# The last group's recurrence, routing and dispatch tables, moved to later steps of the shared expert's loop

## What is computed

```python
x = x + attention(layernorm(x))
x = x + wkv(k=layernorm(x), v=context)       # per channel, a scan over the 128 tokens:
#   q = max(pp, u + k);  y = (exp(pp-q)*aa + exp(u+k-q)*v) / (exp(pp-q)*bb + exp(u+k-q))
h = layernorm(x)
probs = softmax(h @ router_w.T);  top 4 of 16, renormalised
routed = sum over the 4 picks of weight * down_e(silu(h @ gate_e) * (h @ up_e))
shared = silu(h @ sh_gate) * (h @ sh_up) @ sh_down
x = x + routed + sigmoid(h @ sh_gate_w) * shared
```

## Time and profile before

| | us |
|---|---|
| median of 3 runs | 1773.11 (1771.67 to 1774.23) |
| profiled execution, its own time | 1771.54 |
| its span | 1769.7 |
| shared expert's loop on PE | 611.0 to 763.8 |
| tile phase on PE | from 763.76 |

### The profile page before, as it was taken

The page is one execution under the profiler, slowest core; times in us unless marked ns, Lnnn a source line. Parts: engine busy times, 40 slices in busy tenths (PEclk is TensorE's granted clock), DMA queues, the critical chain, the costliest instruction groups (busy, mean ns, idle before and its releaser), DMA issues.

```text
span 1769.7 us, 26015 instructions
## 1 busy us (share of the span) xinstructions
PE 1595.4 (90%) x8599; PEld 1286.9 (73%) x8599; DVE 1115.7 (63%) x2506; ACT 948.8 (54%) x3002; POOL 554.8 (31%) x466
## 2 busy tenths in 40 slices
PE   6999999989998777899999879999879999999766
PEld 4888878878877655667777657777758888888534
DVE  3553675577577576454444475554467888877877
ACT  4666655556665643323323445676836565566556
POOL 2233332464255262411001664446131132211000
PEclk9999999999999988999999878998989999999988
DMA  8043234433354062144433410100031111000001
GB/s 269 27 167 129 95 114 137 158 125 111 123 177 141 22 173 69 60 121 123 130 105 115 146 59 28 34 4 25 1 140 31 33 42 34 12 1 1 1 1 48
DMA packets 85241, 147.33 MB, mean 83 GB/s; under 512 B 9700, under 2 KB 45172, under 8 KB 85108
## 3 DMA queue, kind: packets, MB, share of 16 engines
q1 hardware_dynamic: 78964, 128.89, 22.5%
q0 software_dynamic: 6144, 16.79, 3.0%
HBM read 86.65 MB, written 58.98 MB: 82 GB/s over the span
## 4 chain that ended last, share of the span: by engine, by line
PE 47%; DVE 9%; ACT 3%; issue 3%; POOL 1%; another core or an unknown queue 1%; DVEq 0%; POOLq 0%; ACTq 0%
PE bank L926 5%; PE bank L1163 5%; PE bank L620 4%; PE bank L622 4%; PE bank L944 4%; PE bank L621 4%; PE bank L1043 3%; PE bank L1154 3%; PE bank L1137 3%; PE bank L1025 3%; PE bank L1032 1%; PE bank L1126 1%; PE bank L1145 1%; PE bank L934 1%; PE bank L917 1%
## 5 line engine op out<-in xcount | busy, mean ns | idle before, releaser
L2673 ACT ACTIVATE cross_attention_heads<-cross_attention_heads,small 128x128 f32<-128x128 f32 x256 | 99.6, 390 | 117.7 <-DVE small L2075 117.7
L815 PE MATMUL bank<-self_attention 128*128 128x256 f32 x512 | 127.2, 393 | 21.6 <-ACT self_attention L2409 18.9
L1163 PE MATMUL bank<-cross_attention,cross_attention_heads 128*128 128x256 f32 x512 | 122.1, 381 | 12.8 <-DVE residual L2089 8.2
L2778 POOL CAST qkv_weights_split<-self_attention 128x1024 fp32r<-128x1024 f32 x45 | 51.0, 1133 | 254.8 <-DMA self_attention<-in_wqkv 229.8
L815 PEld LDWEIGHTS bank<-self_attention 128*128 128x128 f32 x512 | 99.5, 198 | 41.3 <-issue 21.7
L2393 ACT ACTIVATE self_attention<-self_attention,small 128x128 f32<-128x128 f32 x256 | 100.2, 394 | 46.6 <-DVE small L1706 43.6
L620 PE MATMUL bank<-x_channel_major,qkv_weights_split 128*128 128x512 f32 x256 | 116.9, 457 | 7.2 <-DVE qkv_weights_split L1739 2.9
L2585 ACT ACTIVATE narrow_late<-bank,small 128x128 f32<-128x128 f32 x256 | 91.2, 376 | 53.3 <-DVE small L1942 52.9
L1163 PEld LDWEIGHTS bank<-cross_attention,cross_attention_heads 128*128 128x128 f32 x512 | 96.0, 190 | 31.2 <-DVE residual L2089 15.1
L2780 POOL TENSOR_TENSOR qkv_weights_split<-self_attention,qkv_weights_split 128x1024 fp32r<-128x1024 f32 x45 | 110.5, 2456 | 3.7
L926 PE MATMUL bank<-experts,tiles 128*128 x316 | 108.0, 465 | 1.8 <-DVE tiles L1816 1.8
(11 more groups left out here) (408 smaller groups left out, 4640.4 us busy)
## 6 DMA issues: line engine op xcount, KB each, us to landing
picked_inputs<-self_attention SPq DMA_DIRECT2D x64, 512.0 KB, 6.3
self_attention<-in_wqkv SPq DMA_DIRECT2D x48, 512.0 KB, 6.1
experts_far<-picked_inputs SPq DMA_DIRECT2D x79, 128.0 KB, 2.1
picked_outputs<-tiles SPq DMA_DIRECT2D x79, 128.0 KB, 1.7
self_attention<-in_wo SPq DMA_DIRECT2D x16, 512.0 KB
experts<-in_moe SPq DMA_DIRECT2D x4, 1408.0 KB
context_values<-context_out SPq DMA_DIRECT2D x16, 256.0 KB
cross_attention<-context_values SPq DMA_DIRECT2D x4, 1024.0 KB, 8.8
```

The costliest lines, as they stand in the source:

```text
L815: m = T.matmul(bank[7][:, 0:D], ZT_a[n % 2][:, h, :], wo_a[p % 2][:, h, :], start=h == 0, stop=h == HG - 1)
L1163: m = T.matmul(bank[7][:, 0:D], ZT_x[n % 2][:, h, :], x_wo[hg % 2][:, h, :], start=h == 0, stop=h == HG - 1)
L2673: m = S.activation(P_x[u][:, h, :], P_x[u][:, h, :], ACT.Exp, bias=negmax_x[u][:, h:h + 1], accum_out=sums_x[u][:, h:h + 1])
```

## The change

Only the numbers of steps between pieces are changed, and on POOL the third scatter of group 2 now stands ahead of the first `wkv_helps`. The work is the same, and so are the units. The core of the diff, on PE, then a line or two of two other engines:

```diff
@@ PE last_group
-                yield from pause(3)
+                yield from pause(6)
                 last_keys(c)
                 yield from pause(5)
                 last_keys(c + 1)
+                yield from pause(6)
+                last_y(c)
+                yield from pause(7)
+                last_y(c + 1)
                 yield from pause(5)
-                last_y(c)
-                yield from pause(5)
-                last_y(c + 1)
-                yield from pause(4)
                 turn_xt(NORM["routing", g], 0)
@@ DVE last_group
                 normalised(NORM["wkv", g])
-                yield from pause(2)
+                yield from pause(5)
                 last_peak(c)
...
                 last_y(c + 1)
-                yield from pause(2)
+                yield from pause(5)
                 last_add(c + 1)
@@ POOL last_group
+                yield from pause(3)
+                scatter(NG - 2, 2)
                 yield from pause(2)
                 wkv_helps(KT * (NG - 1))
-                yield from pause(2)
-                scatter(NG - 2, 2)
```

More of the change, by code:

```diff
@@ L737, in last_group @@
                 logits(g)
-                yield
+                yield from pause(2)
                 turn_logits(g)
-                yield from pause(3)
+                yield from pause(4)
                 count_places(g)
@@ L2354, in last_group @@
                 last_more_exps(c + 1)
-                yield from pause(6)
+                yield from pause(10)
                 both_tables()
@@ L2824, in last_group @@
                 scatter(NG - 2, 1)
+                yield from pause(3)
+                scatter(NG - 2, 2)
                 yield from pause(2)
                 wkv_helps(KT * (NG - 1))
-                yield from pause(2)
-                scatter(NG - 2, 2)
                 yield from pause(3)
                 scatter(NG - 2, 3)
-                yield from pause(2)
+                yield from pause(4)
                 wkv_helps(KT * (NG - 1) + 1)
-                yield from pause(17)
+                yield from pause(21)
                 for b in range(GB):
```

## The result

The changed kernel took 1756.63 us (median of 6, 1751.94 to 1763.60), the kernel before 1772.33 in the same rounds (median of 6, 1770.11 to 1774.23). The ratio of the two is 0.9931, with a 95% interval of 0.9908 to 0.9954: 12 us faster by the ratio, 15.7 by the medians.

What follows compares the result with a forecast made beforehand. PE was taken to set the loop's end, the chain slots, scatter, load having 20.2 us to spare. After: slots 720.2 + 25.4 = tile start 745.6 against 763.76, 18.2 us earlier, so 1755 us; range 1750 to 1766.

Steps and rivals of the forecast that it cites:

- What PE has left after the slots: PE's work between slots and tile phase: 45.6 us before, 20.3 to 25.3 after the change.
- stall as that of unit 19: ACT's late gate near 740 in the kernel before, costing PE 5.0 us; it might or might not come back.
- the rival of the grown stall: Stall near the loop's end at twice 5.0 us: PE ends at 750.5, gain 13.3, 1759.8; chance 0.07.
- What the chain needs: From slots through sixteen scatters to the landed first tile load: unchanged at 25.4 us, now deciding the tile start.
- The slots at 720.2: Date when DVE writes the slots: 2 us later than the 718.19 before, with bounds 717.0 and 726.8.
- The start of the recurrence: DVE's first scan of the recurrence: at 630.3, 1.2 us earlier than before.
- (b): DVE's added products, low parts and sums ahead of the slots: 6.6 us, partly hidden, slots taken 2 later.
- The sum: Tile start 720.2 + 25.4 = 745.6 against 763.76 before: an 18.2 us shift, carried in full to the end.
- the 8.3 for y: PE's waits for y of the recurrence ahead of the slots: 8.3 us go by meeting y of d later.
- second entry: PE's wait for the normalised rows ahead of the slots: 7.5 us, of which 6.5 were to go.

Runs made afterwards that it cites:

- e2: The changed kernel with PE's two transposes of y at steps 17 and 23 instead of 18 and 25; ratio to before 0.9966.
- e4: The changed kernel with picks, slots, tables, count_places and last scatters four steps later on every engine; ratio to before 0.9981.
- e7: The changed kernel with keys, recurrence and y three steps earlier, POOL as before, routing kept at its steps; ratio to before 0.9975.
- e9: The changed kernel with POOL's helps of half c ahead of the third scatter again, fourth scatter at its old step; ratio to before 0.9901.
- e11: The kernel before with y of half d on PE, and all routing behind it on every engine, two steps later; ratio 1.0017.
- e1: The kernel before with the keys and all behind them three steps later on each engine, distances kept; 1742.82 us against 1754.98, ratio 0.9927.
- e8: e1 with both exponentials of d in one ACT unit, DVE's first scan one step later, y of d and routing two later; 1734.04 us, ratio 0.9901.
- e3: The changed kernel with 8 of the last 16 scatters, leaving half of the last group's tokens out of the experts; ratio to before 0.9882.
- e5: The changed kernel, unaltered, profiled on another chip; 1735.29 us against 1754.58, ratio 0.9922.
- e6: The kernel before, unaltered, profiled on the same other chip as e5; 1754.58 us.

## Why the prediction came out as it did

The sign and the path were right, and the time lies in the range: PE set the end of the loop before, 20 us behind the chain slots, scatter, load; the change moved PE's work of some 20 us ahead of the slots; where no late signal disturbs it, the tile phase starts behind the load. That 1755 and 1756.63 lie so close is in part luck. The tile phase moved by 12.3 and not by 18.2, and the two profiled executions differ by as much (1771.54 and 1759.47); the median of the changed kernel lies 2.8 below its profiled execution, where I had set it 1.57 above. Step by step:

- *What PE has left after the slots*, 20.3 to 25.3. On chip B it is 742.37 - 2.76 - 716.61 = 23.0, of which the 20.3 and a new wait of 2.3 for L1775 make 22.6. On the first chip it is 30.0, since a stall as that of unit 19 came for unit 23. So in the profiled execution the rival of the grown stall came true, with a chance of 0.07: it had the tile phase at 750.5 (measured 751.47) and the median at 1759.8 (measured 1756.63, and 1759.47 for this execution).
- *What the chain needs*, 25.4. Measured 742.37 - 716.61 = 25.8 on chip B, and 746.8 - 721.5 = 25.3 on the first. Right, and e2, e4 and e7 end by it.
- *The slots at 720.2.* Measured 721.5, in the bounds. The start of the recurrence was taken at 630.3 and is 630.01. The 2 us for (b) left out POOL's new order, which I had not priced at all: undoing it brings the slots 3.7 us earlier (e9).
- *The sum.* 18.2 forecast, 12.3 on the first chip, 11.7 on chip B. The term that was mis-sized is the stall in the date of before. I set 763.76, with 5.0 us of late signal in it, against a forecast of after without one. With it in both or in neither, 18.2 - 5.0 = 13.2; the slots being 1.1 later against the stage's start and the load 0.4 later against the slots leaves 11.7. The rows were there: the earlier trace rows shows the gate idle 6.37 us with its matmuls long done, and I kept the stall as a cost that the changed kernel might or might not have, but not as one that the kernel before need not have.
- *Where the 20 us came from.* Here the reason was wrong for the largest entry. I wrote that the 8.3 for y go because PE meets y of d four steps behind DVE instead of two. e11 gives that distance to the kernel before and gains nothing; e1 keeps the old distance and gains as much as the change. The wider distance pays only behind the first shift and with the later routing (e2). What paid first is that units 2 and 3 run on PE while the rows are normalised: e7 takes this away (and POOL's new order with it) and keeps the late routing, and the tile phase comes 9.3 us later than in the change. DVE paces the recurrence (18.65 of 20 us busy from 660 to 680), and in the kernel before it stood idle ahead of it, for the product of unit 2 (timeline of DVE, chip B):

```profile
617.09 4.59 DVE L1309 TENSOR_SCALAR normalised_tiles<-residual,small 128x256 f32<-128x256 f32 x4
627.27 0.69 DVE L1767 TENSOR_TENSOR experts<-experts,bank 128x512 f32<-128x512 f32 x1 [5.58 <-issue]
627.88 1.23 DVE L1581 TENSOR_TENSOR_SCAN wkv<-wkv 128x516 f32<-128x516 f32 x1
```

  In e1 two products fill that gap, and the recurrence still starts earlier (18.8 after the stage's start, not 20.5), in the same view:

```profile
619.56 4.63 DVE L1309 TENSOR_SCALAR normalised_tiles<-residual,small 128x256 f32<-128x256 f32 x4
624.11 0.68 DVE L1767 TENSOR_TENSOR experts<-experts,bank 128x512 f32<-128x512 f32 x1
626.80 0.69 DVE L1767 TENSOR_TENSOR experts<-experts,bank 128x512 f32<-128x512 f32 x1 [2.01 <-ACT experts L2471]
628.66 1.70 DVE L1581 TENSOR_TENSOR_SCAN wkv<-wkv 128x516 f32<-128x516 f32 x1 [1.17 <-ACT wkv L2323]
```

  When this scan starts, PE has begun 40 of the loop's matmuls before and 72 in e1: at 0.232 each 7.4 us, and 1.7 for the earlier date, 9.1 of the 11.9 us by which e1's tile phase comes sooner. From there to the end of y of d DVE takes 48.2 us before and 45.6 in e1. From the stage's start to the first tile PE's idle time falls from 29.2 to 18.1. The forecast had this wait for the rows as its second entry, 6.5 us, and missed that over half of the first hangs on it.
- *The later steps of the change*, the wider distances for y and the later routing, have no gain in sum that the ratios show: e1 0.9927, the change 0.9931 and 0.9922. By the medians e1 is 12.2 us below the kernel before, the change 15.7 and 19.3, but on other chips, so that a few us stay open. In the dates what the distances win (e2) the later routing takes away. Together they brought PE's own readiness from 135.8 to 133.3, and the load's from 128.4 to 136.2, and the later of the two counts.
- *The new wait of 5.3 for L1775* was not foreseen. It stands in e1 too (5.1), and e8 took 1.9 of it away with two table loads of ACT fewer and L1775 ahead of the scan.

What is not settled: where the late signal comes from. It (rows of ACT and DVE that wait 4 us or more for "remote" between 700 and 764, or a burst of counts) is in all four profiles whose trace holds only 617 to 664 counts of landed scatters out of 1024, and in none of the seven with all of them (nor in e3, which leaves some out). The chips that show it are those on which the kernel before takes 1771 to 1772 us rather than 1755. Whether the chip, or the recording on it, is at fault no run here tells; the place of the scatters in the program alone does not bring it, by e5 and e6. The ratio of the change agrees on both kinds, 0.9931 and 0.9922.

## What to carry to other kernels

When one engine shows long waits for a piece of another, moving the piece alone may only hand the wait to the next thing in the same queue; look for where the *other* engine stood idle earlier, and put work there. Date both paths that meet at a stage's start: here everything beyond the first three steps moved 2.5 us out of one and 7.8 into the other. And a stall whose cause the profile calls "remote" belongs on both sides of a difference, or on neither.

## What the hardware showed that I had not expected

*A scan that stands still for three POOL instructions.* In the kernel before L1599 of half d takes 5.10 us on the first chip and 5.13 on chip B; in the changed kernel the same scan takes 1.22. Beside the long one POOL runs three instructions without a gap. The timelines of DVE and POOL in the kernel before, then of DVE in the changed one, all on chip B:

```profile
659.14 5.13 DVE L1599 TENSOR_TENSOR_SCAN wkv<-wkv 128x516 f32<-128x516 f32 x1 [1.07 <-ACT wkv L2329]
```
```profile
659.54 1.28 POOL L2893 TENSOR_TENSOR experts_split<-experts,experts_split 128x512 fp32r<-128x512 f32 x1
660.76 1.19 POOL L2786 TENSOR_TENSOR wkv<-wkv 128x512 f32<-128x512 f32 x1
661.90 1.27 POOL L2787 TENSOR_TENSOR wkv<-wkv 128x512 f32<-128x512 f32 x1
```
```profile
659.57 1.22 DVE L1599 TENSOR_TENSOR_SCAN wkv<-wkv 128x516 f32<-128x516 f32 x1
```

1.28 + 1.19 + 1.27 = 3.74, and 5.13 - 1.22 = 3.91. So the stall is the whole length of the three, where I had counted 0.85 for each. In e1 L1599 of half c takes 5.70 beside four POOL instructions, and in the changed kernel L1610 of half c takes 3.57 beside the last two of such a row. In all three cases the scan ends 1.1 us behind the row's end, as if it had stood until POOL was through and then run. The section "Who interferes with whom" of the Trainium skill's page "SBUF — State Buffer" says that a DVE instruction with two inputs in SBUF contends with a GpSimd instruction that reads SBUF, and that who is issued first decides who blocks. The stall agrees with the first half. The order does not show it: the scan above is recorded 0.40 us ahead of POOL's first instruction (659.14 and 659.54) and is still the one that stands; in the changed kernel L2893 begins 0.81 us into the scan (660.38), and nothing stands. Starts on POOL are rough, and the case stays open.

DVE's recurrence was busy 38.2 us before and 34.5 in the change (30 instructions each). That the change is faster by this is not shown: e1 and e9 have a scan of 5.7 us and their slots come earlier than those of the change.

*Counts that PE raises can become visible 5 to 7 us late* beside a long row of scatters, in four of the twelve profiles: 743.15 in that of the changed kernel for matmuls over near 738, 740.09 in that of the kernel before for matmuls over near 733.5. The engines that wait for them stop, and then the granted clock is low as well (0.72 over the 24 us from 740), so that 5.2 us of idleness in the changed kernel cost PE 7.0 between its slots and its tiles (30.0 against 23.0 on chip B).
